# First layer's attention: the context's multiplication by the cosines on POOL, directly behind that by the sines, in place of DVE

## The reference

```python
x = x + tanh(g_xattn[l]) * attention_l(layernorm(x), ctx)
x = x + tanh(g_ffn[l])   * ffn_l(layernorm(x))
```

```python
_rotate_half(x) = concatenate([-x[..., h:], x[..., :h]], axis=-1)      # h = 32
kv_rope = kv_c * cos[None] + _rotate_half(kv_c) * sin[None]
scores  = softmax(q_r . (kv_rope @ W_kr)),  ctx_c = attn @ kv_rope
```

## Time and profile before

| | us |
|---|---|
| median of 3 runs | 3182.2 (3176.74 to 3185.15) |
| profiled execution, own time | 3180.73 |
| its span | 3178.9 |
| stage `attend_short` in it (first POOL work to last store issued) | 70.8 to about 292 |
| one pair of the loop | about 25.65 |
| busy in the whole span: PE, DVE, ACT, POOL | 2781.7, 1970.7, 1531.7, 470.6 |

### The profile page before, as it was taken

The page is one execution under the profiler, slowest core; times in us unless marked ns, Lnnn a source line. Parts: engine busy times, 40 slices in busy tenths (PEclk is TensorE's granted clock), DMA queues, the critical chain, the costliest instruction groups (busy, mean ns, idle before and its releaser), DMA issues. The chain is left out here.

```text
span 3178.9 us, 38552 instructions
## 1 busy us (share of the span) xinstructions
PE 2781.7 (88%) x12773; PEld 2205.7 (69%) x12773; DVE 1970.7 (62%) x3007; ACT 1531.7 (48%) x2192; POOL 470.6 (15%) x350
## 2 busy tenths in 40 slices
PE   6777299779999985997999998699879999995798
PEld 4676199747777764654777776599757777774698
DVE  3563244258888864566888883344347888873444
ACT  3332144237777761213777774344226677771343
POOL 0221033000101110350010111133100010110232
PEclk9556599769999996997999999799868999997899
DMA  1333144363434412013443430233443443420343
GB/s 42 117 152 124 36 110 117 109 169 76 100 86 105 100 40 94 17 54 105 106 95 87 108 92 12 72 118 118 131 141 82 96 98 85 108 61 8 106 117 94
DMA packets 108025, 293.22 MB, mean 92 GB/s; under 512 B 24025, under 2 KB 49577, under 8 KB 106588
## 3 DMA queue, kind: packets, MB, share of 16 engines
q1 hardware_dynamic: 107900, 291.62, 34.6%
HBM read 241.90 MB, written 49.51 MB: 92 GB/s over the span
## 5 line engine op out<-in xcount | busy, mean ns | idle before, releaser
L1083 DVE TENSOR_REDUCE att_top<-banks 128x1 f32<-128x500 f32 x1008 | 670.9, 674 | 223.1 <-PE banks L1026 217.7
L1095 DVE TENSOR_TENSOR att_lo<-att_raw,att_hi 125x896 fp32r<-125x896 f32 x576 | 648.2, 1125 | 51.0 <-ACT att_hi L1139 48.0
L1136 ACT ACTIVATE att_raw<-banks 125x896 f32<-125x896 f32 x576 | 527.7, 916 | 306.6 <-PE banks L1013 302.1
L1043 PE MATMUL banks<-att_hi,att_v 125*66 125x448 f32 x2304 | 564.8, 367 | 0.0
L1139 ACT ACTIVATE att_hi<-banks 125x896 fp32r<-125x896 f32 x576 | 525.8, 913 | 0.0
L1395 PE MATMUL banks<-moe_xs,moe_w 128*128 128x448 f32 x2040 | 446.7, 369 | 69.4 <-DVE moe_xs L1510 67.2
L1026 PE MATMUL banks<-att_kh,att_q 128*128 128x500 f32 x1008 | 420.0, 424 | 55.6 <-DMA att_q<-q_rows 46.2
L1395 PEld LDWEIGHTS banks<-moe_xs,moe_w 128*128 128x128 f32 x2040 | 387.3, 190 | 103.0 <-DVE moe_xs L1510 68.7
L1043 PEld LDWEIGHTS banks<-att_hi,att_v 125*66 125x66 f32 x2304 | 317.2, 138 | 137.2 <-issue 0.4
L1184 POOL TENSOR_TENSOR ctx_ctxT<-att_cu,att_rsb 64x448 f32<-64x448 f32 x96 | 142.7, 1486 | 1408.9 <-DMA att_rsb<-rs_rows 1405.1
L1013 PE MATMUL banks<-att_q,att_kh 128*125 128x448 f32 x1152 | 333.6, 371 | 1.0 <-ACT att_hi L1139 1.0
(11 more groups left out here) (182 smaller groups left out, 2484.2 us busy)
## 6 DMA issues: line engine op xcount, KB each, us to landing
moe_cb<-comb_rows SPq DMA_DIRECT2D x85, 448.0 KB
att_v<-kvn SPq DMA_DIRECT2D x48, 773.4 KB
att_kh<-kvt_hi SPq DMA_DIRECT2D x96, 375.0 KB, 8.4
moe_raw<-L_experts_dram SPq DMA_DIRECT2D x85, 384.0 KB, 6.1
q_rows<-mats_q SPq DMA_DIRECT2D x24, 896.0 KB
att_q<-q_rows SPq DMA_DIRECT2D x48, 448.0 KB, 16.0
att_kl<-kvt_lo SPq DMA_DIRECT2D x48, 375.0 KB, 5.5
kvn<-att_vs SPq DMA_DIRECT2D x8, 1546.9 KB
```

The lines of the kernel that those rows point to most:

```text
L1043: pe.matmul(PS[4 + e][0:DV, 0:HALF], v[:, s % 2, c, part, :], hi[:, u % 3, c % 2, :], start=c == part == 0, stop=False)
L1083: dve.tensor_reduce(top[:, s % 2, n // NS, n % NS:n % NS + 1], PS[6 + (PIECES * s + n) % 2][:, 0:SB], AX.X, ALU.max).then_inc(mx_done, 1)
L1095: dve.tensor_tensor(lo[:, u % 3], raw[:, u % 3], hi[:, u % 3].bitcast(FP32), ALU.subtract).then_inc(dve_low, 1)
L1136: act.activation(raw[:, u % 3], scored, ACT.Exp).then_inc(exp_done, 1)
```

## The change

POOL multiplies by the cosines, in place and directly behind the sines, and DVE no longer does. `place(m - 1)` on POOL now comes after the cosines and waits for them. The wait of `cosines` on `sin_n` is now one of POOL for its own instruction before.

```diff
-    def cosines(self, dve, m, u):
-        dve.wait_ge(self.sin_n, m + 1)
-        dve.tensor_tensor(self.cn[:, u], self.cn[:, u], self.cosN[:, :].unsqueeze(1).broadcast_to([KP, 2, NC * D]),
+    def cosines(self, pool, m, u):
+        pool.wait_ge(self.sin_n, m + 1)
+        pool.tensor_tensor(self.cn[:, u], self.cn[:, u], self.cosN[:, :].unsqueeze(1).broadcast_to([KP, 2, NC * D]),
                           ALU.mult).then_inc(self.cos_n, 1)
...
                         dve.tensor_tensor(p[s], p[s], mx[:, s, :].unsqueeze(2).broadcast_to([128, NT, S]),
                                           ALU.subtract).then_inc(centred, 1)
-                    rot.cosines(dve, m, u)
                     if not first:
                         rot.value_lows(dve, m - 1)
...
                 def step(i, m, u, first, fresh):
                     rot.sines(pool, i, m, u, first)
+                    rot.cosines(pool, m, u)
                     if not first:
-                        pool.wait_ge(rot.sin_n, m + 1)
+                        pool.wait_ge(rot.cos_n, m + 1)
                         place(m - 1)
```

## The result

The changed kernel takes 3189.07 us (median of 20 runs) against 3180.16 for the kernel before, measured beside it: a ratio of 1.0034, 95% interval 1.0025 to 1.0042. That ratio stands for 10.8 us, where 11.8 were forecast; it leaves out two runs of the kernel before that took 7760 and 9830 us, while the two medians, taken over all twenty, are 8.9 us apart. In the profiled executions the span goes from 3178.9 to 3187.4 us.

What follows compares the result with a forecast made beforehand. The second exponential, set by DVE's L779, was taken to bound the loop. 12.2 us lost less 0.4 gained made 11.8 on 3180.73, so 3192.5; the median's 1.5 above gave 3194, own range 3189 to 3200, wider range 3182 to 3208.

Steps and rivals of the forecast that it cites:

- Where the path runs: In the loop, L779 of s = 1 sets the second exponential's start; both come 2.03 us later in pairs 2 to 7.
- The mechanism: L779, with two SBUF inputs, is held for POOL's whole instruction and ends 0.42 us behind it; the waiting one goes next.
- The price of the cosines on POOL: Each added 125x1536 multiplication behind the sines takes 3.43 us, at the least 1.92, after a gap of 0.28 us.
- The term: Second L779 2.03 us late in six pairs, 12.2 us in all; pairs 0 and 1 cost nothing.
- Removal from DVE worth nothing in the loop: Removing eight L206 from DVE gains 0 on the path, except 0.36 us in pair 7, at the value highs.
- POOL twice: Cosines go before the waiting first L779, moving the path 3.7 us a pair: 22 us, 3204; chance 0.12.
- Nothing held, or hidden: L779's 2.25 us have another cause, or POOL's multiplication is much quicker: +0 to +3 us, 3182 to 3185; chance 0.17.
- DVE the bound: PE waits for DVE's list from L779 (s = 1) to L796, so removal gains 22.9 us: 3159; chance 0.05.

Runs made afterwards that it cites:

- the two halves: Changed kernel with POOL's cosines in two instructions of 125x768, one per batch element, at the same place; 1.0011 of the kernel before.
- the subtraction out of PSUM: Changed kernel with masked scores kept in PSUM, so L779 reads one SBUF input and POOL's list is untouched; 0.9986 of the kernel before.
- removal alone: Kernel before with the multiplication by the cosines left out altogether, on neither DVE nor POOL, for timing only; 0.9993 of the kernel before.
- late sines: Changed kernel with POOL's sines, and the cosines and copies behind them, waiting until both subtractions of the pair are through; 0.9986 of the kernel before.

## Why the prediction was right

- **Where the path runs.** The start of the second exponential, set by L779, was named as the place. After, its wait grew by 2.04 us in a pair and the distance of the pairs by the same.
- **The mechanism.** Held for a whole instruction, handed over at its end: the two halves show the hand-over at the end of one instruction, the subtraction out of PSUM shows that the second SBUF input is what is held.
- **The price of the cosines on POOL.** 3.43 us from the sines' row; measured 3.43 alone and 3.63 where they start beside the end of L779. I had left open 0.14 us for that; it was 0.20. But POOL issued them 0.07 us behind the sines (128.14 against 124.63 + 3.44), and not the 0.28 read from the row of the first copy, a wait of the same kind. The two errors cancel: the cosines end 3.70 us behind the sines, where 3.71 was forecast.
- **The term.** 6 x 2.03 = 12.2 us forecast, 6 x 2.04 measured. Pairs 0 and 1 cost nothing: in pair 1 the second L779 takes 2.61 us, but the exponentials follow ACT's value highs with no wait, as before. The end of the stage gave 0.9 us back, and the way from the stage's start to pair 2 was 0.2 us shorter: 11.2 us for the stage in place of 11.8.
- **Removal from DVE worth nothing in the loop.** Shown by removal alone. At the end of the stage I set 0.36 us, the value highs' wait for the store of `vs`. It measured 0.9, and by another wait. The value highs no longer wait, but they were not the last gate: behind them the turned highs L247 waited 2.26 us more for the store of `att_lo`, and still wait 1.75. They start 5.70 us behind the issue of that store before (L188, 277.36) and 4.73 after (287.55). That the earlier store of `vs` brings a gain there was right; the term was too small by half a microsecond. The first line is of the kernel before, the second of the kernel after:

```profile
283.06 0.59 ACT L247 ACTIVATE att_hi<-banks 128x500 fp32r<-128x500 f32 x1 [2.26 <-DMA kvt_lo<-att_lo]
```
```profile
292.28 0.59 ACT L247 ACTIVATE att_hi<-banks 128x500 fp32r<-128x500 f32 x1 [1.75 <-DMA kvt_lo<-att_lo]
```

- **The time itself.** 3189.07 us lies 4.9 below the 3194 of the forecast, at the lower edge of the forecast's own range of 3189 to 3200. Of the 4.9, 2.0 are the start of the sum (3182.2, a median of three runs, against 3180.16 of twenty) and 2.9 the difference of the medians (8.9 for 11.8). The interval of the ratio spans 8 to 13 us, so the stage's 11.2 us is the better test of the sum.
- **POOL twice.** Excluded: the first L779 of pair 2 took 2.25 us after as before, though POOL's next instruction was issued only 0.07 us behind the sines. Even the two halves without a semaphore between them let DVE in.
- **Nothing held, or hidden; DVE the bound.** Both excluded, by a pair of 27.69 us and by the removal alone.

The larger error stood in the expectations of the experiments and not in the forecast: I took the 1.14 us that the second exponential waited as the gain to be had from freeing L779, without asking what PE's transposes of s = 0 would allow. It was 0.44.

## What to carry to other kernels

Moving work between DVE and POOL is not a matter of which has idle time. List what each DVE instruction with two SBUF inputs does while POOL reads SBUF, and see whether one of them is on the path; if so, put POOL's work behind it, cut it into pieces, or let the DVE instruction take an input out of PSUM. Before counting an idle time as a gain, look for the next gate behind it.

## What the runs showed of the hardware

- DVE gets in between two POOL instructions that stand back to back without a semaphore between them (0.99 us for the subtraction beside two halves of 4.11 in all), and between two 0.07 us apart.
- A held instruction counts as busy: L230 is 1.76 us of work and was recorded with 2.10, 3.36 and 4.69, according to what POOL ran beside it. Only a comparison with the same instruction elsewhere shows the hold; no view names POOL as what L779 waited for.
- It holds both ways. With late sines, POOL's sines issued at 131.28, 0.22 us behind L230, took 4.84 us in place of 3.43:

```profile
131.06 1.76 DVE L230 TENSOR_TENSOR att_vs<-att_cr,att_vs 125x1536 fp32r<-125x1536 f32 x1
131.28 4.84 POOL L201 TENSOR_TENSOR att_cm<-att_cn,att_sinN 125x1536 f32<-125x1536 f32 x1 [18.60 <-DVE att_p L779]
```
